# Narrower transposes, splits and reciprocals in the second attention of an audio tower kernel

## The chip, the cores and the metric

The kernel runs on one core of a Trainium2 chip. The metric is the device time of one execution in microseconds. Three runs of the kernel before give a median of 673.44 us (673.26 to 674.73). The engines are named as in the profile: PE is TensorE (PEld its loads of the stationary operand), DVE VectorE, ACT ScalarE, POOL GpSimd, SP SyncE.

## What is computed

The input x is 128 clips of 90 channels and 750 samples. Each clip is cut into 46 patches of 16 samples, embedded to 192 features, and passed through a causal attention of one head and then through an attention of 12 heads of 16 features whose query, key and value projections get a top-2 mixture of 8 low-rank adapters. Cut to what matters here:

```python
h = tok(x, W, b)                                  # (128, 46, 192)
h = h + attn(layernorm(h), Wq, Wk, Wv)            # causal, one head
# second attention, on y = layernorm(h):
qkv = y @ W_qkv.T + b_qkv + adapters(y)           # top 2 of 8, rank 16
q, k, v = split into 12 heads of 16
p = softmax(q @ k.T * 16 ** -0.5)                 # (128, 12, 46, 46)
out = (p @ v) as (128, 46, 192)
return h + out @ W_proj.T + b_proj
```

## The kernel before

The 128 clips are worked on in 16 groups of 8 clips, and within a group in 4 pairs of clips (`PAIRS`). The program of every engine is a loop over 24 steps (`STEPS`). One step holds one instance of every operation, in an order written out by hand at the end of each engine's `step`, and each operation works on the group `s - LAG[op][n]`, so up to nine groups are in flight at different stages. An operation whose group lies outside 0 to 15 is left out: the first steps fill the pipeline, the last ones drain it. The engines run their own lists in order and meet only at semaphores. Products are taken in fp16 with a high and a low part (three matmuls for one product, L1220 to L1222, five in `deep_product`, L1228), so nearly every tensor that is carried from PSUM to SBUF is written twice: its high part by ACT (`copy`, L680), and its low part, source minus high part, by DVE (`low`, L948).

The part that the change touches is the second attention's softmax and its product with the values. For each pair of clips p:

- `s_(p)` (PE, L1424) writes scores with the two clips' queries on partitions 0 to 63 and 64 to 127 (46 of each 64, `SLOT`, are real) and 12 heads of 46 keys in a row.
- `max2`, `shift` (DVE, L959 and L967) and `exp2` (ACT, L720) make the probabilities p2, [128, 12, 64], of which columns 46 to 63 of each head are zero from the start.
- `p_(p)` (PE, L1436): six fp32 transposes of 128 rows by two heads, into the two PSUM banks of ps_p. The operand p2 is the stationary one, the identity the moving one.
- `p2t(p)`: ACT copies ps_p (768 numbers in a row) to p2T's high part in fp16 (L680), then DVE makes its low part (L948). There is one p2T and one ps_p, so PE waits for `p2T_ready` before it transposes the next pair, and `pv(p)` waits for it too.
- `pv(p)` (PE, 18 matmuls at L1220 to L1222): both clips of the pair and a column of ones, so that the sums of the probabilities come with the product.
- `norm2(p)` (DVE): two reciprocals of those sums, one for each clip's 64 rows (L987), then two multiplications into o2 (L991).
- `ot(kh)` (PE, L1466): four fp32 transposes of o2, 128 rows each, for each of two halves; its parts are split as o2T by `o_high` and `o_low`, and go to the projection `pr`.

PE's order around this, from its list of a step (other work between):

```python
p_(3); g_(0); tok(9); g_(1); tok(10); pv(3); at(); tok(11); s_(0); ot(0); sc(); ot(1); s_(1)
qk_(0); qk_(1); qk_(2); p_(0); pt(); cv(0); av(0); av(1); s_(2); pr(0); xt(0); tok(0) ... tok(3); pv(0); p_(1)
```

Ahead of the loop stands a prologue: weights are loaded, transposed and split, and pads and masks are cleared by memsets on DVE and POOL. The last DVE memsets (`v2_room`, L941, and q3's pad, L942) stand directly ahead of step 0. In the prologue p2T serves as the room of a weight product (`qk_T`).

Of the kernel before, what the change touches and what calls it, by code (L numbers as in the profile page):

```python
# [14 lines left out]
NT = T // PATCH  # L15
# [23 lines left out]
RUN = EXTRA  # L39
SLOT = 64  # L40
PAD = 128 - PT_

# [37 lines left out]
def audio_tower(nc, x, tok_W, tok_b, Wq, Wk, Wv, W_qkv, b_qkv, W_gate, b_gate, A, B_lora,  # L80
                W_proj, b_proj, out, scratch):
    with ExitStack() as ctx:
# [118 lines left out]
        s_w = sem("weights_loaded")  # L201
        s_ident = sem("ident_ready")
        s_zero = sem("pads_cleared")
        s_maskf = sem("mask_ready")
# [184 lines left out]
        HP_DMAS = 6  # L389

        def v2_split(n, part):

            return (v2s[:, n, :, :, :, part, 0:HD].rearrange("p s a h e -> p (s a h) e"), heads_of(bank(f"cv{n}")[0:PT_, 0:2 * D]))
# [7 lines left out]
        def _(sp):  # L401
# [35 lines left out]
            def step(s):  # L437
# [40 lines left out]
                def stack_qk():  # L478
                    g = group(s, "stack_qk")
                    if g is not None:  # L480
                        if g == 0:
                            sp.wait_ge(s_wz, 4)
                        sp.wait_ge(s_scw, g * 32 + 32)
                        if g > 1:
                            sp.wait_ge(p_s, (g - 1) * PAIRS)
                        half = SLOT * (g % 2)
                        for n, (qp, kp) in enumerate(((0, 0), (1, 0), (0, 1))):
                            sp.dma_start(q3[half + HD * n:half + HD * (n + 1), :, 0:TG], w_out[g % 2, qp, :, 0:HEADS, :]).then_inc(s_qk3, 16)
                            sp.dma_start(k3[half + HD * n:half + HD * (n + 1), :, :], w_out[g % 2, kp, :, HEADS:2 * HEADS, :]).then_inc(s_qk3, 16)

                def place_v2():
                    g = group(s, "place_v2")
                    if g is not None:
                        if g == 0:
                            sp.wait_ge(s_wz, 4)
                        if g > 1:
# [29 lines left out]
        def _(pool):  # L526
# [23 lines left out]
            pool.wait_ge(s_ident, 1)  # L550
            nc.gpsimd.tensor_copy(ident_b[:], ident[0:PT_, 0:PT_]).then_inc(s_maskf, 1)
            pool.wait_ge(s_maskf, 7)
            for p in range(PAIRS):
# [124 lines left out]
        def _(act):  # L678
# [34 lines left out]
            def step(s):  # L713
# [8 lines left out]
                def p2t(p):  # L722
                    g = group(s, "p2t_high", p)
                    if g is not None:
                        act.wait_ge(p_p, g * PAIRS + (p + 1))
                        if g + p:
                            act.wait_ge(p_pv, g * PAIRS + p)
                        copy(p2T[:, 0].rearrange("p (a b) c -> p a (b c)", a=2), ps_p[:, :, 0:3 * 128]).then_inc(s_p2h, 1)

# [175 lines left out]
        def _(dve):  # L905
# [33 lines left out]


            nc.vector.memset(v2_room, 0.0).then_inc(s_wz, 1)  # L941
            nc.vector.memset(q3[0:SLOT + 3 * HD, :, TG:], 0.0).then_inc(s_wz, 1)  # L942

            def step(s):
# [26 lines left out]
                def p2t(p):  # L971
                    g = group(s, "p2t_low", p)
                    if g is not None:
                        low(p2T[:, 1].rearrange("p (a b) c -> p a (b c)", a=2), ps_p[:, :, 0:3 * 128],
                            p2T[:, 0].rearrange("p (a b) c -> p a (b c)", a=2), 1.0, s_p2h, g * PAIRS + (p + 1), s_p2T)

                def norm2(p):

                    g = group(s, "norm2", p)
                    if g is not None:  # L980
                        dve.wait_ge(p_pv, g * PAIRS + (p + 1))
                        if g:
                            dve.wait_ge(p_ot, g * 2)
                        pv = bank(f"pv{p}")[:, 0:HEADS * 2 * (HD + 1)].rearrange("p (b h e) -> p b h e", b=2, e=HD + 1)
                        for b in range(2):
                            r = slice(SLOT * b, SLOT * (b + 1))
                            nc.vector.reciprocal(rc[r, p, :], pv[r, b, :, HD]).then_inc(s_rc, 1)  # L987
                        for b in range(2):
                            r = slice(SLOT * b, SLOT * (b + 1))
                            dve.wait_ge(s_rc, g * PAIRS * 2 + (2 * p + 1 + b))  # L990
                            nc.vector.tensor_tensor(o2[r, p, 0:D].rearrange("p (h e) -> p h e", h=HEADS), pv[r, b, :, 0:HD],  # L991
                                                    rc[r, p, :].unsqueeze(2).to_broadcast([SLOT, HEADS, HD]),
                                                    ALU.mult).then_inc(s_o2, 1)
# [221 lines left out]
        def _(pe):  # L1215
# [45 lines left out]
            def step(s):  # L1261
# [166 lines left out]
                def p_(p):  # L1428
                    g = group(s, "p", p)
                    if g is not None:  # L1430
# [3 lines left out]
                        for half in range(2):  # L1434
                            for a in range(3):
                                last = nc.tensor.transpose(ps_p[:, half, 128 * a:128 * (a + 1)],  # L1436
                                                           p2[:, 6 * half + 2 * a:6 * half + 2 * a + 2, :].rearrange("p a b -> p (a b)"),
                                                           ident[:])
                        last.then_inc(p_p, 1)
# [17 lines left out]
                def ot(kh):  # L1457
                    g = group(s, "ot", kh)
                    if g is not None:
# [5 lines left out]
                        for p in range(PAIRS):  # L1465
                            last = nc.tensor.transpose(bank(f"ot{kh}")[:, 128 * p:128 * (p + 1)], o2[:, p, DA * kh:DA * (kh + 1)], ident[:])  # L1466
                        last.then_inc(p_ot, 1)
# [63 lines left out]


def f32_of(ap):

# [33 lines left out]
```

## Time and profile before

| | us |
|---|---|
| median of 3 runs | 673.44 (673.26 to 674.73) |
| the profiled execution's own time | 675.54 |
| its span, first to last instruction | 673.8 |
| PE busy | 602.9 (89% of the span) |
| DVE busy | 509.0 (76%) |
| POOL busy | 380.8 (57%) |
| ACT busy | 367.0 (54%) |
| mean granted TensorE clock | 0.953 of full speed |

The lists of the engines repeat every 34.0 us in the middle of the span, so the span falls into a prologue (to about 57 us), steps that fill the pipeline (to about 157 us), full steps (to about 558 us), and steps that drain it. In a row of the trace, "a<-b" is what is written and what is read (buffer numbers left out), the shapes are partitions x elements per partition, and for a matmul the form "128*128 128x128" gives rows and columns of the stationary operand and then rows and columns of the moving one. "Idle before" is how long the engine stood still just ahead of the instruction, and the arrow names what ended that.

### The profile page before, as it was taken

Reading aid. Unit: us, or ns where it says so; the run is one execution under the profiler, and the core shown is the slowest. Engines: PE = TensorE matmul, PEld = TensorE weight load, DVE = VectorE, ACT = ScalarE, POOL = GpSimd, SP = SyncE. Lnnn points to the kernel's source line nnn. Section 1 sums busy time; section 2 is a strip of 40 time slices with the busy share of each in tenths; the row PEclk is TensorE's granted clock in tenths of the full one; section 3 lists DMA queues with packets and bytes.
Section 4 is the critical chain, followed back from the end, with each engine's and each line's share of the span. In section 5 each row is a group of like instructions: output and inputs, shape, how many; then the busy total and the mean of one; then the engine's idle time right before and its main releaser. Section 6 shows DMA issues by size and latency. Waiting matters only on the chain.

```text
span 673.8 us, 20478 instructions
## 1 busy us (share of the span) xinstructions
PE 602.9 (89%) x7805; PEld 537.4 (80%) x7805; DVE 509.0 (76%) x1369; ACT 367.0 (54%) x688; POOL 380.8 (57%) x649
## 2 busy tenths in 40 slices
PE   1597779989999999999999999999999998877673
PEld 1367668879898989898989898989898987766563
DVE  4324145677888888888888888888888888887772
ACT  2524455556666666666666666666666454533231
POOL 5608768876767676767666666767675323121100
PEclk9999779998999999999999999999999998987876
DMA  8843564968494949494949494949492616161500
GB/s 207 148 94 82 120 149 96 156 171 138 124 159 136 159 134 159 135 159 135 150 141 155 138 166 128 173 123 167 131 167 65 108 32 104 36 105 37 94 23 17
DMA packets 74930, 82.94 MB, mean 123 GB/s; under 512 B 10093, under 2 KB 60241, under 8 KB 74833
## 3 DMA queue, kind: packets, MB, share of 16 engines
q1 hardware_dynamic: 74832, 81.63, 59.5%
q8 instruction: 62, 1.02, 0.7%
q14 instruction: 36, 0.29, 0.2%
HBM read 50.24 MB, written 13.57 MB: 95 GB/s over the span
## 4 chain that ended last, share of the span: by engine, by line
PE 78%; DVE 7%; POOL 6%; SPq 4%; issue 3%; ACT 1%; DMA 0%; POOLq 0%; DVEq 0%; ACTq 0%
PE ps_r L1228 23%; PE ps_tok L1220 7%; PE ps_tok L1221 6%; PE ps_tok L1222 6%; PE ps_p L1436 6%; PE ps_s L1424 4%; PE ps_r L1220 4%; PE ps_r L1222 4%; SPq L403 4%; PE ps_r L1221 4%; PE ps_r L1466 3%; PE ps_r L1346 3%; POOL xs L588 3%; PE ps_r L1289 2%; PE ps_r L1359 1%
## 5 line engine op out<-in xcount | busy, mean ns | idle before, releaser
L588 POOL TENSOR_TENSOR xs<-raw,xs 90x368 f16<-90x368 f32 x192 | 163.9, 881 | 19.8 <-ACT xs L680 19.8
L1220 PE MATMUL ps_tok<-w_tok,xs 128*128 128x192 f16 x576 | 146.2, 254 | 1.2 <-DVE h L1003 1.2
L1221 PE MATMUL ps_tok<-w_tok,xs 128*128 128x192 f16 x576 | 145.9, 253 | 0.0
L1222 PE MATMUL ps_tok<-w_tok,xs 128*128 128x192 f16 x576 | 145.8, 253 | 0.0
L680 ACT ACTIVATE p2T<-ps_p 128x768 f16<-128x768 f32 x64 | 51.8, 810 | 72.3 <-PE ps_p L1436 57.5
L680 ACT ACTIVATE xs<-raw 90x736 f16<-90x736 f32 x96 | 75.6, 805 | 0.1
L596 POOL TENSOR_TENSOR ad<-ga,disp 128x384 f32<-128x384 f32 x16 | 13.4, 839 | 105.8 <-DVE disp L1058 105.8
L588 POOL TENSOR_TENSOR xe<-raw,xe 90x368 f16<-90x368 f32 x64 | 55.6, 881 | 28.2 <-ACT xe L680 28.2
L1220 PEld LDWEIGHTS ps_tok<-w_tok,xs 128*128 128x128 f16 x576 | 66.8, 116 | 4.2 <-POOL xs L588 1.1
L1221 PEld LDWEIGHTS ps_tok<-w_tok,xs 128*128 128x128 f16 x576 | 66.8, 116 | 1.7
L1222 PEld LDWEIGHTS ps_tok<-w_tok,xs 128*128 128x128 f16 x576 | 66.8, 116 | 0.3
L948 DVE SCALAR_TENSOR_TENSOR p2T<-ps_p,p2T 128x768 f16<-128x768 f32 x64 | 60.7, 949 | 3.9 <-ACT p2T L680 2.9
L1220 PE MATMUL ps_r<-v,p2T 128*128 128x68 f16 x384 | 46.7, 202 | 16.2 <-DVE p2T L948 14.2
L1436 PE MATMUL ps_p<-ident,p 128*128 128x128 f32 x384 | 56.7, 287 | 2.4 <-DVE p2T L948 2.0
L1220 PEld LDWEIGHTS ps_r<-v,p2T 128*128 128x128 f16 x384 | 38.7, 101 | 17.6 <-DVE p2T L948 16.0
L987 DVE RECIPROCAL rc<-ps_r 64x12 f32<-64x12 f32 x128 | 29.5, 230 | 30.6 <-PE ps_r L1222 27.0
L991 DVE TENSOR_TENSOR o<-ps_r,rc 64x192 f32<-64x192 f32 x128 | 45.5, 356 | 4.0
L1436 PEld LDWEIGHTS ps_p<-ident,p 128*128 128x128 f32 x384 | 44.8, 147 | 4.3 <-issue 2.7
L1222 PE MATMUL ps_r<-v,p2T 128*128 128x68 f16 x384 | 46.8, 201 | 0.0
L1221 PE MATMUL ps_r<-v,p2T 128*128 128x68 f16 x384 | 46.8, 201 | 0.0
L967 DVE TENSOR_TENSOR df<-ps_s,mx 128x552 f32<-128x552 f32 x64 | 46.2, 722 | 0.7
L959 DVE TENSOR_REDUCE mx<-ps_s 128x12 f32<-128x552 f32 x64 | 46.1, 720 | 0.2 <-PE ps_s L1424 0.2
(163 smaller groups left out, 1614.0 us busy)
## 6 DMA issues: line engine op xcount, KB each, us to landing
raw<-x SPq DMA_DIRECT2D x32, 1035.0 KB, 7.9
qk_scratch<-qk SPq DMA_DIRECT2D x32, 276.0 KB, 3.0
q<-qk_scratch SPq DMA_DIRECT2D x48, 138.0 KB, 7.0
k<-qk_scratch SPq DMA_DIRECT2D x48, 138.0 KB, 7.7
xs<-xe SPq DMA_DIRECT2D x32, 184.0 KB
v<-v2s SPq DMA_DIRECT2D x64, 73.3 KB
out<-h2b SPq DMA_DIRECT2D x16, 276.0 KB
xs<-xe SPq DMA_DIRECT2D x16, 149.5 KB
```

The costliest lines, as they stand in the source:

```text
L588: nc.gpsimd.tensor_tensor(lo, src, hi, ALU.subtract).then_inc(s_lo, 1)
L680: return nc.scalar.activation(out_, in_, ACT.Copy, scale=scale)
L948: nc.vector.scalar_tensor_tensor(out=out_, in0=src, scalar=scale, in1=hi, op0=ALU.mult, op1=ALU.subtract).then_inc(done, 1)
L959: nc.vector.tensor_reduce(mx[:].rearrange("p (a h) -> p a h", a=2), scores2(), AX_X, ALU.max).then_inc(s_mx, 1)
L967: nc.vector.tensor_tensor(df[:].rearrange("p (a h) k -> p a h k", a=2), scores2(), mx[:].rearrange("p (a h) -> p a h", a=2).unsqueeze(3).t ...
L987: nc.vector.reciprocal(rc[r, p, :], pv[r, b, :, HD]).then_inc(s_rc, 1)
L991: nc.vector.tensor_tensor(o2[r, p, 0:D].rearrange("p (h e) -> p h e", h=HEADS), pv[r, b, :, 0:HD], rc[r, p, :].unsqueeze(2).to_broadcast([ ...
L1220: mm(dst, stat[0], mov[0], start=start, stop=False)
L1221: mm(dst, stat[0], mov[1], start=False, stop=False)
L1222: return mm(dst, stat[1], mov[0], start=False, stop=stop)
L1228: last = mm(dst, stat(a), mov(b), start=start and n == 0, stop=stop and n == 4)
L1436: last = nc.tensor.transpose(ps_p[:, half, 128 * a:128 * (a + 1)], p2[:, 6 * half + 2 * a:6 * half + 2 * a + 2, :].rearrange("p a b -> p ( ...
```

## The change

The 46 rows of each clip stand at partitions 0 to 45 and 64 to 109, so the last real row is 109 of 128; ROWS is 64 + 46 = 110. The change does four things:

1. The transposes `p_` and `ot` take 110 rows in place of 128. The stationary operand keeps its 128 columns; the moving identity shrinks from 128 to 110 columns.
2. `p2t` splits only the 46 used of each 64 columns: 12 x 46 = 552 numbers per partition in place of 768, on ACT and on DVE. DVE's instruction becomes a plain subtraction. The columns that are no longer written are cleared once in the prologue, by a DVE memset of p2T, and ACT waits for it (`s_wz` of 3).
3. `norm2` takes one reciprocal over 110 rows for both clips, and multiplies 46 rows for each clip. The column of ones stands in the values of both clips, so the sums in the first clip's block of `pv` are those of every row, and the one reciprocal reads that block alone.
4. o2's rows 46 to 63, which are now read by `ot` but never written, are cleared once by a POOL memset in the prologue, and DVE waits for it.

```diff
+ROWS = SLOT + NT
...
+        def p2T_used(part):
+
+            return used(p2T[:, part].rearrange("p (a b) (c q) -> p a (b c) q", a=2, q=SLOT))
+
+        def ps_p_used():
+            return used(ps_p[:, :, 0:3 * 128].rearrange("p a (b q) -> p a b q", q=SLOT))
...
             nc.gpsimd.tensor_copy(ident_b[:], ident[0:PT_, 0:PT_]).then_inc(s_maskf, 1)
+            nc.gpsimd.memset(o2[:], 0.0).then_inc(s_o2z, 1)
...
                         act.wait_ge(p_p, g * PAIRS + (p + 1))
+                        act.wait_ge(s_wz, 3)
                         if g + p:
                             act.wait_ge(p_pv, g * PAIRS + p)
-                        copy(p2T[:, 0].rearrange("p (a b) c -> p a (b c)", a=2), ps_p[:, :, 0:3 * 128]).then_inc(s_p2h, 1)
+                        copy(p2T_used(0), ps_p_used()).then_inc(s_p2h, 1)
...
+            nc.vector.memset(f32_of(p2T[:]), 0.0).then_inc(s_wz, 1)
             nc.vector.memset(v2_room, 0.0).then_inc(s_wz, 1)
...
-                        low(p2T[:, 1].rearrange("p (a b) c -> p a (b c)", a=2), ps_p[:, :, 0:3 * 128],
-                            p2T[:, 0].rearrange("p (a b) c -> p a (b c)", a=2), 1.0, s_p2h, g * PAIRS + (p + 1), s_p2T)
+                        dve.wait_ge(s_p2h, g * PAIRS + (p + 1))
+                        nc.vector.tensor_tensor(p2T_used(1), ps_p_used(), p2T_used(0), ALU.subtract).then_inc(s_p2T, 1)
...
+                        nc.vector.reciprocal(rc[0:ROWS, p, :], pv[0:ROWS, 0, :, HD]).then_inc(s_rc, 1)
+                        dve.wait_ge(s_rc, g * PAIRS + (p + 1))
+                        dve.wait_ge(s_o2z, 1)
                         for b in range(2):
-                            r = slice(SLOT * b, SLOT * (b + 1))
-                            nc.vector.reciprocal(rc[r, p, :], pv[r, b, :, HD]).then_inc(s_rc, 1)
-                        for b in range(2):
-                            r = slice(SLOT * b, SLOT * (b + 1))
-                            dve.wait_ge(s_rc, g * PAIRS * 2 + (2 * p + 1 + b))
+                            r = slice(SLOT * b, SLOT * b + NT)
                             nc.vector.tensor_tensor(o2[r, p, 0:D].rearrange("p (h e) -> p h e", h=HEADS), pv[r, b, :, 0:HD],
-                                                    rc[r, p, :].unsqueeze(2).to_broadcast([SLOT, HEADS, HD]),
+                                                    rc[r, p, :].unsqueeze(2).to_broadcast([NT, HEADS, HD]),
                                                     ALU.mult).then_inc(s_o2, 1)
...
-                                last = nc.tensor.transpose(ps_p[:, half, 128 * a:128 * (a + 1)],
-                                                           p2[:, 6 * half + 2 * a:6 * half + 2 * a + 2, :].rearrange("p a b -> p (a b)"),
-                                                           ident[:])
+                                last = nc.tensor.transpose(ps_p[:, half, 128 * a:128 * a + ROWS],
+                                                           p2[0:ROWS, 6 * half + 2 * a:6 * half + 2 * a + 2, :].rearrange("p a b -> p (a b)"),
+                                                           ident[0:ROWS, 0:ROWS])
...
-                            last = nc.tensor.transpose(bank(f"ot{kh}")[:, 128 * p:128 * (p + 1)], o2[:, p, DA * kh:DA * (kh + 1)], ident[:])
+                            last = nc.tensor.transpose(bank(f"ot{kh}")[:, 128 * p:128 * p + ROWS], o2[0:ROWS, p, DA * kh:DA * (kh + 1)],
+                                                       ident[0:ROWS, 0:ROWS])
...
+def used(ap):
+    return ap[..., 0:NT]
```

Two waits of SP on `s_wz` go from 4 to 5, for the memset that was added. No instruction changes its place in an engine's list. On DVE, at the end of a full step, the list before reads (rc and o are the reciprocals and the normalised output of `norm2`, the rows from lg to disp the router's ranking and dispatch):

```order
L948 SCALAR_TENSOR_TENSOR p2T<-ps_p,p2T 128x768
L1003 SCALAR_TENSOR_TENSOR h<-ps_tok,b_tok_bc 128x192
L1032 TENSOR_TENSOR lg<-ga,b_gate_bc 128x24
L1034 TENSOR_REDUCE top<-lg 128x3
L1035 TENSOR_TENSOR lgm<-lg,top 128x24
L1041 TENSOR_TENSOR ahead<-lg 128x192
L1043 TENSOR_TENSOR over<-ahead,beats 128x192
L1045 TENSOR_REDUCE rank<-over 128x24
L987 RECIPROCAL rc<-ps_r 64x12 x2
L991 TENSOR_TENSOR o<-ps_r,rc 64x192 x2
```

and the list of the changed kernel at the same place:

```order
L987 TENSOR_TENSOR p2T<-ps_p,p2T 128x12x46
L1014 SCALAR_TENSOR_TENSOR h<-ps_tok,b_tok_bc 128x192
L1043 TENSOR_TENSOR lg<-ga,b_gate_bc 128x24
L1045 TENSOR_REDUCE top<-lg 128x3
L1046 TENSOR_TENSOR lgm<-lg,top 128x24
L1052 TENSOR_TENSOR ahead<-lg 128x192
L1054 TENSOR_TENSOR over<-ahead,beats 128x192
L1056 TENSOR_REDUCE rank<-over 128x24
L997 RECIPROCAL rc<-ps_r 110x12
L1002 TENSOR_TENSOR o<-ps_r,rc 46x192 x2
```

The neighbours stay; one reciprocal is gone, and the split is of 552 numbers.

## Rows read from the trace of the kernel before

**Rows 1.** The page: engines' busy time, and TensorE's granted clock in 40 slices
```profile
PE 602.9 (89%) x7805; PEld 537.4 (80%) x7805; DVE 509.0 (76%) x1369; ACT 367.0 (54%) x688; POOL 380.8 (57%) x649
...
PEclk9999779998999999999999999999999998987876
```

**Rows 2.** Windows: us, busy (x count) of PE, PEld, DVE, ACT, POOL, clock, DMA
```profile
157.00:558.00 401.00, 399.94 (x5660) 365.42 (x5657) 354.00 (x975) 254.33 (x476) 262.52 (x443) 1.00 0.66 136
562.00:674.00 112.00, 80.77 (x1058) 68.96 (x1058) 79.87 (x183) 38.22 (x69) 14.70 (x22) 0.81 0.33 58
```

**Rows 3.** Waits, 562 to 674 us: us in total, times, longest us
```profile
PE ps_r L1220 <- DVE p2T L948: 14.2, 7, 3.4
...
DVE rc L987 <- PE ps_r L1222: 8.5, 9, 1.3
```

**Rows 4.** The chain that ended last, 562 to 674 us: shares by line
```profile
by line: PE ps_r L1228 14.4%; PE ps_p L1436 9.2%; DVE p2T L948 8.6%; PE ps_r L1466 6.2%; issue 6.2%; PE ps_r L1220 5.2%; DVE o L991 4.7%; PE ps_r L1222 4.3%; PE ps_r L1221 4.2%; DVE rc L987 4.1%; PE ps_s L1424 3.4%; POOL xn L629 1.7%; PE ps
```

**Rows 5.** The chain, 200 to 300 us: start us, us, what
```profile
278.40 0.46 PE ps_r L1466 x4
...
297.85 0.32 PE ps_r L1359 x4
...
298.92 0.66 PE ps_p L1436 x6
```

**Rows 6.** Groups by form, 157 to 562 us: xcount | busy us, mean ns
```profile
L1436 PE MATMUL ps_p<-ident,p 128*128 128x128 f32 x288 | 40.0, 275 | 0.0
...
L1466 PE MATMUL ps_r<-ident,o 128*128 128x128 f32 x96 | 15.3, 282 | 0.0
```

**Rows 7.** Groups by form, the whole span
```profile
L948 DVE SCALAR_TENSOR_TENSOR p2T<-ps_p,p2T 128x768 f16<-128x768 f32 x64 | 60.7, 949 | 3.9 <-ACT p2T L680 2.9
...
L680 ACT ACTIVATE p2T<-ps_p 128x768 f16<-128x768 f32 x64 | 51.8, 810 | 72.3 <-PE ps_p L1436 57.5 <-PE ps_r L1222 13.5
...
L967 DVE TENSOR_TENSOR df<-ps_s,mx 128x552 f32<-128x552 f32 x64 | 46.2, 722 | 0.7
...
L991 DVE TENSOR_TENSOR o<-ps_r,rc 64x192 f32<-64x192 f32 x128 | 45.5, 356 | 4.0
...
L720 ACT ACTIVATE p<-df 128x552 f32<-128x552 f32 x64 | 42.0, 657 | 0.0
...
L987 DVE RECIPROCAL rc<-ps_r 64x12 f32<-64x12 f32 x128 | 29.5, 230 | 30.6 <-PE ps_r L1222 27.0
...
L1003 DVE SCALAR_TENSOR_TENSOR h<-ps_tok,b_tok_bc 128x192 f32<-128x192 f32 x48 | 16.7, 349 | 19.3 <-PE ps_tok L1222 19.2
```

**Rows 8.** Groups by form, 562 to 674 us
```profile
L987 DVE RECIPROCAL rc<-ps_r 64x12 f32<-64x12 f32 x32 | 7.3, 229 | 9.1 <-PE ps_r L1222 8.5
```

**Rows 9.** The chain, 640 to 674 us: start us, us, what
```profile
651.79 0.23 DVE rc L987
...
652.05 0.25 DVE rc L987
...
656.59 0.82 ACT p2T L680
...
657.43 0.97 DVE p2T L948
```

**Rows 10.** Timeline to 62 us: start us, us, instruction [idle before]
```profile
15.01 1.73 POOL L588 TENSOR_TENSOR xe<-raw,xe 90x368 f16<-90x368 f32 x2 [5.91 <-ACT xe L680]
...
54.72 2.78 DVE L941 MEMSET v<- 128x3264 f32 x1 [0.63 <-issue]
...
58.28 0.36 DVE L1003 SCALAR_TENSOR_TENSOR h<-ps_tok,b_tok_bc 128x192 f32<-128x192 f32 x1 [0.55 <-PE ps_tok L1222]
...
59.08 0.18 DVE L1016 BATCH_NORM_AGGREGATE mv<-st 128x2 f32<-128x6 f32 x1
...
58.79 0.25 PE L1220 MATMUL ps_tok<-w_tok,xs 128*128 128x192 f16 x1 [0.54 <-DVE h L1003]
...
61.84 0.19 POOL L566 TENSOR_TENSOR ve<-mv,eps 128x1 f32<-128x1 f32 x1
```

More of the change, by code:

```diff
@@ L202, in audio_tower @@
         s_ident = sem("ident_ready")
+        s_o2z = sem("o2_cleared")
         s_zero = sem("pads_cleared")
@@ L481, in stack_qk @@
                         if g == 0:
-                            sp.wait_ge(s_wz, 4)
+                            sp.wait_ge(s_wz, 5)
                         sp.wait_ge(s_scw, g * 32 + 32)
@@ L494, in place_v2 @@
                         if g == 0:
-                            sp.wait_ge(s_wz, 4)
+                            sp.wait_ge(s_wz, 5)
                         if g > 1:
```

## The prediction

> **What bounds the kernel now.** I read the page first. PE is busy for 89% of the span and DVE for 76%, and TensorE's clock is at full speed from about a fifth of the span to nine tenths of it, below that only at both ends [rows 1]. Shares over the whole span do not say where an edit pays, so I read the windows next. From 157 to 558 us PE is busy for 399.94 of 401 us at clock 1.00, while DVE is busy for 354 and ACT for 254 [rows 2]. There PE's own list is the limit, and only what shortens PE shortens the kernel. From 562 to 674 us PE is busy for 80.77 of 112 us at a mean clock of 0.81, and DVE for 79.87: neither fills the time [rows 2]. The waits of that stretch say why: PE stood 14.2 us in seven waits for DVE's p2T, and DVE 8.5 us in nine waits for PE's product before a reciprocal [rows 3]. So the drain is a chain p_, high part on ACT, low part on DVE, pv, reciprocal, and each link counts. The chain that ended last gives the links their weight in these 112 us: transposes p_ 9.2% and ot 6.2%, DVE's p2T 8.6%, reciprocals 4.1% [rows 4].
>
> **Part 1, the transposes.** In the full steps PE works back to back, so what counts is the spacing from one instruction to the next, which the chain shows, not an instruction's own length, which overlaps its neighbours. Six p_ transposes take 0.66 us, 110 ns each with 128 moving columns, and four ot transposes 0.46 us, 115 ns each. The transposes of xn2 (L1359) are the same kind of instruction, fp32 with a stationary operand of 128 columns, but 92 rows and so 92 moving columns: four take 0.32 us, 80 ns each [rows 5]. From 128 to 92 is 36 columns for 30 ns, 0.83 ns a column; 18 columns fewer give 15 ns. For one instruction the ends are nothing (the spacing is set by the stationary load) and the whole step to the 92-column row, 30 ns. I take 15, because 110 lies halfway between two rows of the same kind; the 30 would need the whole step to come in its first half. Between 157 and 562 us there are 288 p_ and 96 ot transposes [rows 6]: 384 x 15 ns = 5.8 us, all of it on the path, for PE has no idle time to give. In the drain the chain holds (9.2% + 6.2%) of 112 us = 17.2 us of transposes [rows 4], part of it at half clock, where a column costs twice as much; 18 of 128 columns of that are 2.4 us.
>
> One rule speaks against this part. The Trainium skill, TensorE: Matmul & The Clock Gate, section Back-to-back issue gap, says that in a stream of weight loads and matmuls the spacing is set by both, and its section on LDWEIGHTS lets a load take as long as the stationary operand has columns, by its formula 107 ns for 128 of them. The stationary operand keeps its 128 columns here, so by that rule this part would give nothing, and the sum below would be 4.2 us in place of 12.0. The trace is against it, since the 92-column transposes have 128 stationary columns and still follow each other at 80 ns [rows 5]; I keep the row's price and make the rule's case a rival.
>
> **Part 2, the split on 552 numbers.** DVE's low part takes 949 ns for 768 numbers. A DVE subtraction that reads 552 fp32 numbers from PSUM takes 722 ns [rows 7]. I take 722 for the new one: 227 ns less. ACT's high part takes 810 ns for 768; the nearest ACT row with 552 numbers in runs of 46 is exp2's, 657 ns [rows 7]: 153 ns less. That exp2 costs so little with its output in runs of 46 is also why I charge nothing for runs. In the full steps both gains are worth nothing: PE is never kept waiting there [rows 2]. What covers them is PE's own list; without that cover DVE would be the next limit, at 354 of 401 us. In the drain the chain holds 8.6% of 112 = 9.6 us of DVE's low parts [rows 4]; 227 of 949 of that is 2.3 us. ACT's high parts are on the chain twice (the row at 656.59 is one of the two) [rows 9]: 0.3 us.
>
> **Part 3, one reciprocal.** A reciprocal on 64 rows x 12 takes 230 ns; it runs over the free dimension, and rows cost nothing: DVE's h<-ps_tok on 128 rows x 192 takes 349 ns, the o multiplication on 64 rows x 192 takes 356 ns [rows 7]. So one on 110 rows takes 230 ns, the multiplications on 46 rows keep their 356 ns, and of the drain's 32 reciprocals 16 are dropped [rows 8]. On the chain they stand as two pieces in a row, 0.23 and 0.25 us [rows 9], 4.1% of 112 = 4.6 us in all [rows 4]; half of it is 2.3 us. The first multiplication now directly follows the reciprocal that it needs. Before, the second one stood so too, and no gap of more than 0.03 us separates the chain's pieces there, so I charge nothing. In the full steps this is covered as in part 2.
>
> **Part 4, the memsets.** DVE clears 128 x 3264 fp32 in 2.78 us, 0.85 ns an element, so p2T's 768 take 0.65 us, just ahead of step 0. DVE then stood idle 0.55 us until PE's first embedding tile was done, so h is late by 0.1 us, and PE, which waited 0.54 us for it, starts its next tile as much later. The next who needs it is POOL, whose layer norm at 61.84 us comes after its own queue of splits and reads what DVE had at 59.3 us [rows 10]. Ends: nothing and 0.65 us; I take nothing. POOL's memset of o2, 1024 elements, costs some 0.9 us by the same price, ahead of a wait of 5.91 us for the first input [rows 10]: nothing. SP's waits for one more count and ACT's and DVE's new waits are for memsets of the prologue, 90 us before the first p_, and nobody queues behind them.
>
> **The sum.** Full steps 5.8 us. Drain 2.4 + 2.3 + 0.3 + 2.3 = 7.3 us if every link of the chain gives all it has. It will not: where a link is shortened another path comes up, for instance DVE's mx or h2b pieces that already stand directly ahead of a low part. I take 85%, 6.2 us; the ends are 1 us (other paths take over at once) and 7.3 us. In all 12.0 us. The profiled execution has a span of 673.8 and its own time is 675.54; less 12.0 that is 661.8 and 663.5. The median of the runs lies 2.1 us below the profiled one, so I forecast 673.44 - 12.0 = **661.4 us**.
>
> **Rivals.**
> - *The drain is held by something else.* Layer norm 2 on POOL, ACT's copies and half-clock PE stretches are in the same 112 us. Then the full steps' 5.8 us and 1 us remain: 666.6 us. Against: seven waits for p2T itself. Chance 0.11.
> - *The stationary load sets the transposes' spacing.* Parts 2 and 3 alone, 85% of 4.9 us: 673.44 - 4.2 = 669.2 us. For it: nothing but that the stationary operand stays at 128 columns; against: the 80 ns row. It is the case that the Trainium skill's rule above describes. Chance 0.08.
> - *The change doesn't do what it says on the split:* the pattern of 2 x 6 runs of 46 costs ACT and DVE as much as 768 in a row. Then 2.6 us of the drain go, 85% of it 2.2 us: 663.6 us. Against: exp2 writes the same runs. Chance 0.04.
> - *Slower: TensorE's clock in the drain.* The granted clock there is 0.81 on average, that is a mix of 2.4 and 1.2 GHz, in a stretch where PE often stands waiting. The PE entries named in the chain's row add up to 47% of it, 52 us [rows 4], or 52 x 0.81 = 42 us of work at full clock. If the new rhythm of waits lowers the mean to c, that work takes 42/c. It eats the whole 12 us at c = 0.66 and leads to 677 us at 0.62. For it: the last tenth of the span already has 0.6 and 0.7 in places [rows 1]. Against: the change shortens the very stretches in which PE waits. Chance 0.03.
>
> **How the numbers follow.** My forecast has 0.74, with its own range from 657 to 665: 13.1 us if the drain gives all, and a few us more if the drain's clock rises (42/0.88 is 4 us less than 52). A run of this kernel can tell about 0.2%, 1.35 us, from no change. Everything but the last rival is faster by more than that: faster 0.95, within 0.2% 0.02 (a partial form of the last rival), slower 0.03. For the range I go from 657 to 669.5, which takes in the first three rivals and leaves out the last, the outer tails and the 30 ns end of part 1 (653 us).
>
> **What would show it.** In the profile after: a p_ group spaced at 0.57 us and an ot group at about 0.40 us on the chain; a period of 33.5 us in place of 34.0 with PE still busy all through; DVE's p2T near 722 ns and ACT's near 650; 64 reciprocals of 110x12 at 230 ns; the wait of PE for p2T in the drain down from 14.2 by some 3 us. An unchanged period would prove the stationary-load rival, a shorter period with an unchanged 112 us drain the first one. I would be wrong altogether if PE showed idle time in the full steps, or a clock below 1.00 there.

## The result, and the profile after

| | before | after |
|---|---|---|
| median, us | 673.35 (670.48 to 674.73, 4 runs) | 662.52 (661.36 to 664.97, 4 runs) |
| ratio after / before, 95% interval | | 0.9849 (0.9807 to 0.9892) |
| the profiled execution's own time | 675.54 | 661.36 |
| its span | 673.8 | 659.6 |
| mean granted clock | 0.953 | 0.956 |

The forecast was 661.4 us with a range from 657.0 to 669.5; the kernel takes 662.5. It is faster by 10.8 us, where 12.0 were expected. Below are the rows of the changed kernel that answer to [rows 1 to 7, 10].

The page of the changed kernel, busy time and granted clock:

```profile
PE 592.3 (90%) x7805; PEld 527.3 (80%) x7805; DVE 484.4 (73%) x1306; ACT 356.0 (54%) x688; POOL 382.0 (58%) x650
...
PEclk9999789998999999999999999999999999996875
```

PE is 10.6 us less busy for the same 7805 instructions, DVE 24.6 us less for 63 fewer (64 reciprocals less, one memset more). Taken over the whole span, DVE's saving is more than twice what the kernel gained. Where it counted only the stretches tell.

Windows of the changed kernel, full steps and then drain, with the columns of [rows 2]:

```profile
157.00:552.00 395.00, 393.46 (x5639) 359.51 (x5637) 335.29 (x926) 245.93 (x476) 261.29 (x442) 1.00 0.67 137
556.00:660.00 104.00, 76.78 (x1055) 64.39 (x1051) 72.71 (x167) 35.55 (x69) 14.35 (x22) 0.80 0.35 62
```

PE is still busy for 99.6% of the full steps at clock 1.00, so its list is the limit there as before. DVE's share fell from 88% to 85%, and the period doesn't follow it (e2, e3 and e4 below).

Chain of the changed kernel in full steps (start us, us, what), which answers to [rows 5]:

```profile
291.99 0.32 PE ps_r L1370 x4
...
295.69 0.57 PE ps_p L1447 x6
...
308.82 0.40 PE ps_r L1477 x4
```

Six p_ transposes are spaced 95 ns apart where it was 110, four ot 100 where it was 115; xn2's, which the change doesn't touch, still take 80.

Groups by form, whole span (busy us, mean ns | idle before):

```profile
L1447 PE MATMUL ps_p<-ident,p 110*128 110x110 f32 x384 | 49.6, 267 | 1.8 <-DVE p2T L987 1.2 <-ACT p L730 0.4
L987 DVE TENSOR_TENSOR p2T<-ps_p,p2T 128x552 f16<-128x552 f32 x64 | 46.3, 723 | 3.1 <-ACT p2T L690 2.2
L1002 DVE TENSOR_TENSOR o<-ps_r,rc 46x192 f32<-46x192 f32 x128 | 45.5, 355 | 4.2
L690 ACT ACTIVATE p2T<-ps_p 128x552 f16<-128x552 f32 x64 | 40.3, 630 | 64.3 <-PE ps_p L1447 53.1 <-PE ps_r L1233 10.3
```

The split on DVE costs 723 ns (949 before), on ACT 630 (810 before); the multiplication costs the same on 46 rows as on 64. The reciprocal on 110 rows has 64 instructions of 232 ns, 14.8 us in all.

Waits in the drain, 556 to 660 us (us in total, times, longest), beside [rows 3]:

```profile
PE ps_r L1231 <- DVE p2T L987: 11.1, 7, 3.1
...
DVE rc L997 <- PE ps_r L1233: 7.5, 8, 1.3
```

**Where the time went.** As a milestone I take the first reciprocal of the first attention (`rl`, DVE) in each step: it has one fixed place in DVE's list, so the distance from one to the next is the period of a step, and the milestones cut the span into fill, twelve full steps, and drain. The same cut is used for every kernel below.

| us, in the profiled executions | before | after |
|---|---|---|
| start to the third milestone | 149.7 | 147.9 |
| twelve full steps | 408.6 | 404.0 |
| period of an undisturbed full step | 33.88 | 33.42 |
| drain | 115.5 | 107.7 |
| span | 673.8 | 659.6 |

The period is 0.46 us shorter, which is 5.5 us over twelve steps. (The 34.0 us named ahead of the prediction are 33.88 when measured this way.) Twelve periods are less than the second line: in every kernel the first of the twelve steps and the eleventh take 0.8 to 1.6 us longer than the period (in one kernel, with filler, the first takes 3.3 us longer). Two things in the table are scatter and no effect: the first line varies between 147 and 150 us among all kernels with no order to it, and other single steps take 0.3 to 2 us longer (more in the last section). So the profiled pair shows 14.2 us, while the medians show 10.8.

### The profile page after: what moved, and what is told of

Same layout as the page of the kernel before. It is cut to its first block, busy times and chain, and to the rows that moved or that the text cites. A ratio compares the mean times of both kernels' runs of the same rounds, so it can differ in the third digit from the quotient of the medians.

```text
span 659.6 us, 20481 instructions
## 1 busy us (share of the span) xinstructions
PE 592.3 (90%) x7805; PEld 527.3 (80%) x7805; DVE 484.4 (73%) x1306; ACT 356.0 (54%) x688; POOL 382.0 (58%) x650
## 4 chain that ended last, share of the span: by engine, by line
PE 77%; DVE 7%; POOL 5%; SPq 4%; issue 3%; ACT 2%; DMA 0%; POOLq 0%; DVEq 0%
PE ps_r L1239 24%; PE ps_tok L1231 7%; PE ps_tok L1232 7%; PE ps_tok L1233 7%; PE ps_p L1447 5%; PE ps_s L1435 4%; PE ps_r L1231 4%; SPq L412 4%; PE ps_r L1233 4%; PE ps_r L1232 4%; PE ps_r L1357 3%; POOL xs L598 2%; PE ps_r L1477 2%; PE ps_r L1300 2%; PE ps_r L1370 1%
## 5 line engine op out<-in xcount | busy, mean ns | idle before, releaser
L690 ACT ACTIVATE p2T<-ps_p 128x552 f16<-128x552 f32 x64 | 40.3, 630 | 64.3 <-PE ps_p L1447 53.1
L1231 PE MATMUL ps_r<-v,p2T 128*128 128x68 f16 x384 | 45.8, 200 | 13.4 <-DVE p2T L987 11.1
L1447 PE MATMUL ps_p<-ident,p 110*128 110x110 f32 x384 | 49.6, 267 | 1.8 <-DVE p2T L987 1.2
L1231 PEld LDWEIGHTS ps_r<-v,p2T 128*128 128x128 f16 x384 | 38.1, 100 | 14.4 <-DVE p2T L987 12.8
L987 DVE TENSOR_TENSOR p2T<-ps_p,p2T 128x552 f16<-128x552 f32 x64 | 46.3, 723 | 3.1 <-ACT p2T L690 2.2
L1002 DVE TENSOR_TENSOR o<-ps_r,rc 46x192 f32<-46x192 f32 x128 | 45.5, 355 | 4.2
L850 ACT ACTIVATE xn<-h,nb,rs 128x192 f32<-128x192 f32 x48 | 26.1, 543 | 40.1 <-POOL nb L621 40.1
L1239 PE MATMUL ps_r<-x2T,w_qk 128*128 128x368 f16 x240 | 46.9, 327 | 0.0
L1233 PE MATMUL ps_r<-v,p2T 128*128 128x68 f16 x384 | 45.8, 199 | 0.0
L1232 PE MATMUL ps_r<-v,p2T 128*128 128x68 f16 x384 | 45.7, 199 | 0.0
```

Of the source, the lines that this page charges most:

```text
L690: return nc.scalar.activation(out_, in_, ACT.Copy, scale=scale)
L987: nc.vector.tensor_tensor(p2T_used(1), ps_p_used(), p2T_used(0), ALU.subtract).then_inc(s_p2T, 1)
L1231: mm(dst, stat[0], mov[0], start=start, stop=False)
L1232: mm(dst, stat[0], mov[1], start=False, stop=False)
L1233: return mm(dst, stat[1], mov[0], start=False, stop=stop)
L1239: last = mm(dst, stat(a), mov(b), start=start and n == 0, stop=stop and n == 4)
```

## Experiments

Every ratio is to the kernel before, run beside it on the same chip. The medians of before were 672.9 us (24 runs) beside e1, e2, e3 and e4, 674.4 (11 runs) beside a1, e7, e8 and f12, and 673.9 (26 runs) beside the rest. "Gain" below is the ratio applied to 673.4 us. The first question is how the gain is divided among the parts, since my sum gave each of them a size.

### e1: the transposes alone

```diff
-    transpose(ps_p[:, half, 128 * a:128 * (a + 1)], p2[:, ...], ident[:])
+    transpose(ps_p[:, half, 128 * a:128 * a + ROWS], p2[0:ROWS, ...], ident[0:ROWS, 0:ROWS])
-    transpose(bank(f"ot{kh}")[:, 128 * p:128 * (p + 1)], o2[:, ...], ident[:])
+    transpose(bank(f"ot{kh}")[:, 128 * p:128 * p + ROWS], o2[0:ROWS, ...], ident[0:ROWS, 0:ROWS])
```

The split stays at 768 numbers and there are two reciprocals, now on 46 rows each; o2 and ps_p are cleared once.

> The transposes of part 1 alone (p_ and ot on 110 rows); the split stays on 768 numbers and there are two reciprocals, on 46 rows each; ps_p and o2 are cleared once in the prologue. My theory (PE's list is the limit of the full steps, a column costs 0.83 ns): the period falls from 33.9 to 33.4 us, the stretch up to the drain shrinks by about 6 us and the drain by about 2 us, median about 665.5 us. Rival (the stationary load sets the spacing): period and median unchanged, 673.3 us. Rival (the drain's gain came from DVE alone): 6 us, all of it before the drain, about 667.5 us.

Measured: 670.87 us (7 runs), ratio 0.9948 (0.9924 to 0.9972), a gain of 3.5 us. The period is 33.42 us, all of the change's 0.46. The drain takes 114.7 us, hardly less than before. The 665.5 us expected before the run are missed by 5.4.

### e2: the split alone

```diff
-    copy(p2T[:, 0]..., ps_p[:, :, 0:3 * 128])
+    copy(p2T_used(0), ps_p_used())
-    low(p2T[:, 1]..., ps_p[:, :, 0:3 * 128], p2T[:, 0]..., 1.0, ...)
+    nc.vector.tensor_tensor(p2T_used(1), ps_p_used(), p2T_used(0), ALU.subtract)
...
```

Transposes on 128 rows, two reciprocals on 46 rows.

> Part 2 alone: the split on 552 of 768 numbers, its memset and waits; transposes on 128 rows, two reciprocals, on 46 rows each. My theory: DVE's 227 ns and ACT's 180 ns a pair are hidden in the full steps, so the period stays at 33.9 us, and the drain gives about 2.2 us: median about 671.1 us. Rival (DVE's time counts everywhere): 64 x 0.227 = 14.5 us, 659 us. Rival (the drain is held by other paths): 673.3 us.

Measured: 669.27 us (12 runs), ratio 0.9937 (0.9911 to 0.9962), a gain of 4.2 us (1.7 either way). Period 33.88 us, as before; drain 109.8 us.

### e3: the reciprocal alone

```diff
+    nc.vector.reciprocal(rc[0:ROWS, p, :], pv[0:ROWS, 0, :, HD])
     for b in range(2):
-        nc.vector.reciprocal(rc[r, p, :], pv[r, b, :, HD])
...
```

> Part 3 alone: one reciprocal on 110 rows, multiplications on 46 rows; transposes and split as before. My theory: period unchanged, about 2.0 us from the drain, median about 671.4 us. Rival (DVE's time counts everywhere): 64 x 0.23 = 14.7 us, 658.7 us. Rival (the wait for the one reciprocal, which no second one covers any more, gives it back): 673.3 us or a little over.

Measured: 672.03 us (12 runs), ratio 0.9984 (0.9962 to 1.0006), a gain of 1.1 us that its interval doesn't tell from none. Period 33.88 us; the profiled execution, 1.8 us below this kernel's median, has a drain of 109.7.

### e4: split and reciprocal together, transposes as before

> Parts 2 and 3 together, so the whole change but the transposes. My theory: period unchanged, 4.2 us from the drain (5 if the two add up without loss), median about 669.2 us, and the difference to the changed kernel, 662.5 us, is the transposes' 6.7. Rival (the parts shorten the same link twice, or another path takes over): no more than the larger of parts 2 and 3 alone, about 671 us.

Measured: 668.24 us (6 runs), ratio 0.9922 (0.9892 to 0.9953), a gain of 5.3 us, which is e2's and e3's together. Period 33.88 us, drain 108.6.

### a1: the changed kernel again

> The changed kernel once more, unedited, beside the others of this call. Additive parts would put it at the transposes' step of the first call (0.52% less than before) plus that of parts 2 and 3 (0.78%): 1.30%, 664.2 us. If the parts help each other (the transposes alone lengthened the half-clock time of the drain, the split takes it back), it is below that: 1.5% as measured at first, 662.8 us.

Measured: 663.14 us (6 runs), ratio 0.9841 (0.9804 to 0.9878), a gain of 10.7 us; period 33.42, drain 107.4 us. The result repeats. The parts add up to 8.8 us (e1's 3.5 and e4's 5.3), or to 10.1 with e1's repeat below (4.8). The intervals are 1.6 to 2.5 us either way, so they don't tell whether the parts merely add or help each other.

### e0: the memsets and their waits alone

```diff
+    nc.vector.memset(f32_of(p2T[:]), 0.0).then_inc(s_wz, 1)
     nc.vector.memset(v2_room, 0.0).then_inc(s_wz, 1)
...
+    nc.gpsimd.memset(o2[:], 0.0).then_inc(s_o2z, 1)
```

> The kernel before with the two new memsets and their waits alone (p2T cleared by VectorE 0.70 us before the loop, o2 by POOL 0.95 us). Theory, as in the prediction: no change, 672 to 675 us, since xt waits for weights that come at 71.5 us and VectorE's first h, though 0.8 us later, is done long before. Rival: the later start of VectorE goes through to the end, 0.84 us, 0.1 per cent; then the first rl of the first step comes 0.8 us later and the time is 0.8 us more, which the interval of such a run would hardly tell, but the milestones of the trace would.

Measured: 674.83 us (10 runs), ratio 1.0005 (0.9977 to 1.0033). The timeline of this kernel's prologue (start us, us, instruction):

```profile
54.71 0.70 DVE L944 MEMSET p2T<- 128x768 f32 x1
...
59.20 0.36 DVE L1008 SCALAR_TENSOR_TENSOR h<-ps_tok,b_tok_bc 128x192 f32<-128x192 f32 x1
```

The first h starts 0.92 us later than in [rows 10]. Its first milestone is at 91.84 us, where before had 93.26, but that milestone lies anywhere between 91.2 and 93.3 us in the kernels of this document, so it can't show what became of a delay of this size. The ratio shows no cost, with an interval of 1.9 us either way. This kernel does before's work otherwise, so it is also a second look at before: its drain took 113.7 us, against 115.5. So two profiled drains of the same work can differ by 1.8 us. Of that, 1.5 us lie in the drain's first step, which took 30.76 us here at a granted clock of 1.00 and 32.27 us in before at 0.95.

### What became of the transposes' share in the drain

e1's drain was 0.8 us shorter in the profile, where I had counted on 2.0, and its median left the drain no gain at all (3.5 us, with 5.5 from the full steps). The clock was one suspect, since e1's last stretch ran at 0.71 of full speed and before's at 0.76. I repeated e1 beside a kernel that differs from it by matmuls that nobody needs:

```diff
+    if s >= 19 and k in (3, 7, 8, 10):
+        pe.wait_ge(s_h, GROUPS * 3)
+        for _ in range(12):
+            mm(ps_tok[:, 0:D], xs[:, 0, 0, 0, 0:128, 0], w_tok[:, 0, 0, :], start=True, stop=True)
```

The moving operand of these matmuls has 192 columns (`D`); the text before the run says 96.

> The kernel with the narrower transposes alone, and 12 more matmuls of 96 columns at four of the tok slots of every step from the 19th on, on data that has long been there. Their result is overwritten by the tok matmuls that follow, so nothing of the output changes. The question is why the transposes alone gave 3.5 us of the 7.8 expected. Theory A, the granted clock: with less for TensorE to do in the drain, the clock stays low for longer there and takes back what the transposes give. Then this kernel's drain shows a higher clock than that of the transposes alone (0.71 in its last 84 us), its last stretch is shorter than 84.1 us by some 2 to 4 us, and the time is 667 to 668, if the filler's own work (48 matmuls a step of about 0.05 us, of which part lies in waits) does not eat it. Theory B, the drain of the transposes alone is bound by the wide split on VectorE, and the clock has no part: the last stretch stays at 84 us or grows by the filler's work, and the time is 671 to 673.

> The transposes p_ and ot on 110 rows alone, once more, beside the one with filler on the same chip. Expected as before: 0.9948 of the kernel before, 670 to 671 us; full steps of 33.42 us, and a last stretch of 83 to 85 us at a clock near 0.71. If the last stretch comes out at 79 to 80 us instead, at a clock of 0.76 or more, then the small gain of the first run was scatter of the clock, and no lasting trait of this kernel; the time is then 666 to 667.

Measured: with filler 668.92 us (12 runs), ratio 0.9938 (0.9915 to 0.9961); without it 669.22 us (9 runs), ratio 0.9929 (0.9896 to 0.9962). The windows of the drain, cut at its first whole step, without and with filler (clock third from the end):

```profile
552.62:584.71 32.09, 27.26 (x373) 22.79 (x372) 28.14 (x72) 16.60 (x33) 6.81 (x12) 0.95 0.42 74
584.71:667.30 82.59, 54.64 (x728) 46.38 (x726) 55.54 (x128) 23.87 (x41) 8.41 (x12) 0.73 0.29 53
```

```profile
554.88:586.76 31.88, 28.31 (x385) 24.15 (x384) 27.94 (x71) 16.63 (x33) 6.79 (x12) 0.95 0.42 73
586.76:670.10 83.34, 69.12 (x956) 60.73 (x954) 55.56 (x128) 23.86 (x41) 8.43 (x12) 0.88 0.30 53
```

The filler adds 228 matmuls and 14.5 us of busy PE to the last stretch and lifts the clock from 0.73 to 0.88, and the stretch is 0.75 us longer, not 2 to 4 us shorter. PE's wait for p2T falls from 13.8 to 5.0 us with it: part of the filler lies in that wait. That is theory B's outcome in the trace, though its 671 to 673 us were not measured, and the medians don't tell the two kernels apart.

What it rules out is that a higher clock, bought in this way, returns anything. It doesn't decide whether the clock ate the transposes' share, for the filler has a price of its own. In the chain of this kernel's last stretch it stands with 5.5 us ahead of the last output (and 5.9 us more beside the writing of it), yet the stretch grew by only 0.75 us. By that estimate the rest of it is 4.7 us shorter, which the higher clock would explain. More numbers point to the clock. e1's 16 executions ran at a mean clock of 0.938 to 0.956, before's 61 beside all the runs at 0.951 to 0.963. Twice (1 - clock) times the span is an estimate of the time at half clock, and gives 67 to 71 us for e1, 58 to 59 for before, and 41 for e1 with filler. PE's busy time in the last stretch didn't fall with the narrower transposes: 56.7 and 54.6 us in e1's two traces, at 0.71 and 0.73, against 55.5 in before and 55.3 in e0, at 0.76 and 0.74. And the drain's first step, with the same work, took 30.59 us in e1's first trace, at 1.00, and 32.09 us in its repeat, at 0.95, as with e0 and before.

The same filler on the changed kernel:

> The changed kernel with 12 matmuls of 192 columns, whose result nobody reads, ahead of pv(0), pv(2), pv(3) and behind pv(1) in steps 19 to 23, where PE otherwise stands waiting. Clock theory (the transposes' gain in the drain is eaten because a PE with less to do runs at half clock for longer): the mean clock rises from 0.956 to 0.97 or more, the 78 us at 0.74 become 72 or so, median about 657 us in spite of the added work. Rival (the drain's length is set by DVE's and ACT's work, the clock is a bystander): the filler only delays PE, 662.5 to 668 us.

Measured: 662.74 us (6 runs), ratio 0.9832 (0.98 to 0.9864), the changed kernel's own time, at a clock of 0.85 in the last stretch in place of a1's 0.77. In the profiled pair that stretch is 3.3 us longer with filler (81.4 against 78.1), so here too nothing speaks for it. This profiled execution is the slowest of its six, 2.7 us above their median, and that of e1 with filler is 2.9 us above its own.

The other candidate is in the chain. Here is the drain's chain of e1's repeat, by line:

```profile
by line: PE ps_r L1233 14.5%; DVE p2T L952 9.2%; PE ps_p L1442 6.5%; issue 6.4%; DVE o L996 5.3%; PE ps_r L1225 5.0%; DVE rc L992 4.4%; PE ps_r L1472 4.4%; PE ps_r L1227 4.2%; PE ps_r L1226 4.0%; PE ps_s L1429 2.8%; DVE mx L963 2.3%; DVE h 
```

and here the waits of PE for p2T in the drain in it, in e2 and in the changed kernel run again:

```profile
PE ps_r L1225 <- DVE p2T L952: 13.8, 7, 3.5
```

```profile
PE ps_r L1232 <- DVE p2T L986: 12.0, 7, 3.2
```

```profile
PE ps_r L1231 <- DVE p2T L987: 11.1, 7, 3.1
```

Summed up by engine from the pieces of each drain's chain:

| us on the chain of the drain | PE | DVE | drain |
|---|---|---|---|
| before | 57.0 | 38.1 | 115.5 |
| e0 | 54.3 | 39.1 | 113.7 |
| e1 | 53.3 | 41.6 | 114.7 |
| e1, again | 50.4 | 43.8 | 114.7 |
| e2 | 52.5 | 36.8 | 109.8 |
| e3 | 54.1 | 35.8 | 109.7 |
| e4 | 54.9 | 32.7 | 108.6 |
| after | 49.2 | 36.7 | 107.7 |
| a1 | 50.3 | 35.6 | 107.4 |

With narrower transposes PE's part of the chain shrinks, and DVE's grows in its place: p2T, mx and df stand on it longer. PE's wait for p2T stays at 14 us (13.8, beside [rows 3]) and shrinks only where the split is narrower. From e4 to after it is the same trade: PE 5.7 us less, DVE 4.0 more. I read this as two paths of nearly equal length, one through PE's transposes and one through DVE's list, with DVE's the longer: DVE's savings come through and PE's mostly don't. Against the mean of before and e0, 114.6 us, e1 saves nothing, and the transposes on top of e4 save about 1 us. That reading is argued from the chains and not shown: no run holds the clock and changes the path, or the other way round. So whether the second path or the lower clock took the transposes' share, or both, stays open.

### e7: the stationary operand narrowed too

The rival of the stationary load is tested here. p_ takes 110 columns of p2 as the stationary operand in place of 128, and the split runs on 110 partitions.

```diff
-    transpose(ps_p[:, half, ...], p2[0:ROWS, ...].rearrange("p a b -> p (a b)"), ident[0:ROWS, 0:ROWS])
+    transpose(ps_p[0:ROWS, half, ...], p2[0:ROWS, ...].rearrange("p a b -> p (a b)")[:, 0:ROWS], ident[0:ROWS, 0:ROWS])
```

> The changed kernel with 110 in place of 128 columns in the stationary operand of p_ (and the split on 110 partitions). My theory (the moving columns set the spacing): a group of six stays at 0.57 to 0.59 us and the period at 33.42 us, the median at 662.5. Rival (the stationary load still sets part of it): down to 0.50 us a group, a period shorter by up to 0.3 us, median down to 659 us.

Measured: 662.18 us (4 runs), ratio 0.9835 (0.9792 to 0.9878), a1's time. Groups by form of this kernel:

```profile
L1447 PE MATMUL ps_p<-ident,p 110*110 110x110 f32 x384 | 49.8, 268 | 1.0 <-ACT p L730 0.4 <-DVE p2T L987 0.3
...
L1447 PEld LDWEIGHTS ps_p<-ident,p 110*110 110x110 f32 x384 | 39.5, 138 | 2.9 <-issue 1.1 <-ACT p L730 0.5
```

The load is named 138 ns instead of 145 and the spacing is still 0.57 us for six; the period is 33.40 us. The width of the stationary operand doesn't set it. Whether it is the moving columns or the rows (both went from 128 to 110) wasn't tried: the identity of a transpose is square, so the two can't be parted here.

### e8: pv in two passes

PE waits in the drain for the low part, while two thirds of pv's matmuls need only the high part. This kernel starts those first:

```diff
-    pe.wait_ge(s_p2T, g * PAIRS + (p + 1))
+    pe.wait_ge(s_p2h, g * PAIRS + (p + 1))
...
+        for part in range(2):
+            mm(dst[:, :, 2 * j:2 * j + 2, :], p2T[:, 0, j, :], v2[:, g % 2, :, :, p, j, part, :], start=j == 0 and part == 0, stop=False)
+    pe.wait_ge(s_p2T, g * PAIRS + (p + 1))
+    for j in range(HEADS // 2):
+        mm(dst[:, :, 2 * j:2 * j + 2, :], p2T[:, 1, j, :], v2[:, g % 2, :, :, p, j, 0, :], start=False, stop=j == HEADS // 2 - 1)
```

> The changed kernel with pv in two passes: the 12 matmuls that need only p2T's high part go ahead of the wait for the low part, the 6 with the low part behind it. If the chain p_, high, low, pv, reciprocal bounds the drain: of 7 waits of PE for p2T each is shorter by up to the 0.4 us (0.65 at half clock) of the 12 matmuls, so the drain gives 2 to 4 us, and the full steps nothing: median about 659.5 us. If what that wins is lost to the clock as with the transposes alone: no change, 662.5 us.

Measured: 661.16 us (660.54 to 661.78, 6 runs), ratio 0.9811 (0.9783 to 0.9838). That is 2.0 us below a1 beside it; the intervals overlap, but the drain is also shorter, 104.5 us against 107.4, so I take it for a gain. It falls short of the 659.5 us that were expected. The wait on the low part and the chain of this kernel's drain:

```profile
PEld ps_r L1466 <- DVE p2T L987: 4.6, 7, 2.0
```

```profile
by line: PE ps_r L1239 17.0%; DMA v<-v2s 7.4%; issue 6.9%; PE ps_p L1447 5.7%; SPq L510 5.2%; DVE p2T L987 4.6%; DVE o L1002 3.9%; PE ps_s L1435 3.0%; PE ps_r L1462 2.5%; PE ps_r L1479 2.4%; DVE h L1105 2.3%; PE ps_r L1466 2.2%; DVE st L111
```

The load's wait for the low part is 4.6 us where the changed kernel's was 12.8. That isn't 8 us won: the load now also waits 4.6 us, in five waits, for the high part from ACT, which the old order hid behind the low part, so 3.6 us of waiting are gone and 2.9 us come out of the drain. The DMA that places v2, with its queue on SP, has come up as a new link (12.6% of the chain), where it had no place before.

### e9: e8 and the other transposes with spare rows

xt and at take their second tile on 112 rows instead of 128.

> The changed kernel with two more edits: pv starts its matmuls on the high parts before it waits for the low parts (the edit of e8_two_pass_pv), and the transposes xt and at take their second tile on its 112 rows instead of 128. Of these there are 9 calls a step, one of the three tiles of each 16 moving columns narrower: 9 x 16 x 0.83 ns = 0.12 us a step by the 0.83 ns a column that the two widths of p_ and ot showed, which is 1.9 us over 16 steps. If the list of TensorE sets the full steps, the period goes from 33.42 to 33.30 us and the time from 661.2 to 659.5 us, 0.978 of before. If the spacing of these calls is set by what they wait for, the period stays at 33.42 and the time at 661.

Measured: 661.02 us (6 runs), ratio 0.9805 (0.9774 to 0.9836), e8's time. Its drain took 105.8 us, 1.6 less than a1's where e8's was 2.9 less, so what the two passes save in a profiled drain is known no better than that. The text before the run counted three times too many: only one tile in three is narrower, two of xt's six transposes in a step and one of at's three, which makes 3 x 16 x 0.83 ns = 0.04 us a step. The period is 33.40 us against 33.42, but e7, without this edit, has 33.40 too, so the 0.04 us can't be read from it. e8 and e9 are the best of all that ran; between them the runs don't decide.

## Why the prediction was right, point by point

- **Full steps, 5.8 us expected, 5.5 shown.** The period fell by 0.46 us for 32 transposes, 14.4 ns each against the 15 that I took between the two rows of [rows 5]. It falls by that (in e7 and e9 by 0.48) in each kernel with narrower transposes, and stays at 33.88 us in each without. PE is still busy throughout.
- **Splits and reciprocals nothing in the full steps.** Right: e2, e3 and e4 have before's period.
- **The drain, 6.2 us expected in all.** The medians leave 10.8 - 5.5 = 5.3 us for it; the profiled pair shows 7.8, of which up to 1.8 is scatter by e0. The total was right and its division wrong, so there is luck in the total. The transposes' term, 2.4 us before the cut to 85%, was too big: e1's two medians give 3.5 and 4.8 us for the whole kernel (1.6 and 2.2 either way), less than the full steps alone. The splits' term of 2.6 us (DVE's 2.3, ACT's 0.3) looks too small: e2 gives 4.2 us, though its interval goes down to 2.5. The reciprocals' 2.3 us looks too big, though it lies within e3's interval: e3 gives 1.1 (1.5 either way), and from e2 to e4 it is 1.1 again. The step that failed is the reading of [rows 4] as a price list. The chain's shares say what each link holds, and not what shortening it returns. Why the transposes returned less, a DVE path beside them or the lower clock, is open. e2's executions ran at a higher clock than before's beside it (0.957 to 0.965 against 0.951 to 0.963), which may be how the split returned more than its share. My cut of 15% was the right idea, spread over the wrong terms.
- **Durations.** DVE's split at 722 ns came out at 723, ACT's at 657 came out at 630, the reciprocal at 230 at 232, the multiplication unchanged. On DVE runs of 46 cost nothing extra (723 ns, and 722 for the subtraction of [rows 7]), and rows nothing either (232 ns on 110, 230 on 64).
- **The waits.** PE's for p2T fell from 14.2 to 11.1 us, the 3 that were named.
- **The memsets.** They cost nothing that e0's ratio shows, as was forecast. I wrote that h would be late by 0.1 us, since DVE had stood idle 0.55 us ahead of it, waiting for PE's first embedding tile. In the changed kernel it came 0.84 us later, with 0.60 us of idle time still ahead of it:

```profile
54.18 0.70 DVE L952 MEMSET p2T<- 128x768 f32 x1
...
58.52 0.32 PE L1233 MATMUL ps_tok<-w_tok,xs 128*128 128x192 f16 x1
...
58.83 0.25 PE L1233 MATMUL ps_tok<-w_tok,xs 128*128 128x192 f16 x1
...
59.12 0.36 DVE L1014 SCALAR_TENSOR_TENSOR h<-ps_tok,b_tok_bc 128x192 f32<-128x192 f32 x1 [0.60 <-PE ps_tok L1233]
```

  But the memset isn't what made it late. PE's tile was late: its last matmul ended at 59.08 us (58.25 in before), because PE's matmuls stood 0.16 us apart, at half clock, until 58.67 us, and in before only until 56.93; from there they stand 0.08 us apart. In the kernels with the same memsets whose clock rose early (56.82 us in e8, 56.13 in e4), h follows the memsets with no idle time, at 58.53 and 58.29 us against 58.28 in before. So the idle time was slack, and the memset of 0.70 us used it up, about as the prediction had it. Behind it there is more: the first transposes of xt start at 71.46 us in the changed kernel, and at 71.50 in before.
- **The rival of the stationary load** fell: by it the ratio would have been 0.9937, and the period unchanged. The Trainium skill, TensorE: Matmul & The Clock Gate, section Back-to-back issue gap, sets the spacing of a stream of loads and matmuls by both; by its formula, an estimate, 128 stationary columns would hold these transposes at 107 ns. The trace doesn't agree: with 128 stationary columns they stand 95 ns apart, and with 110 (e7) the same.
- **The rival of a drain held by something else** fell as a whole, since the drain did get shorter, but for one part of three, the transposes, something else did hold it. **The flat pattern** fell with the 723 ns. **The clock** was 0.74 in the last stretch against 0.76 and didn't make the kernel slower; what it took from the transposes is the open question above.

## What to carry to other kernels

Cut the span by a milestone that comes once a step and read each stretch for itself: in the full steps only the list of the engine that never waits counted, and in the drain DVE's narrower split counted and PE's narrower transposes hardly. A chain's share is no price for a link: here one link returned less than its share promised and another, by its median, more. Before pricing it, look for the path that runs beside it and for what the shorter work does to TensorE's clock, and repeat the profile, since two drains of the same work differ. When a consumer waits for the last of several inputs, as pv did for the low part, order its work so that what needs the earlier inputs goes first, and expect the next links (here the high part from ACT, and a DMA) to take part of the gain.

## What was unexpected

- **fp32 transposes are priced by the 128, 110 or 92 on their moving side, and finely:** 110, 95 and 80 ns apart, 0.83 ns for each column, the same whether the stationary operand has 128 or 110 columns.
- **Lone stalls of PE in the full steps.** A step now and then takes 0.3 to 2 us more than its period. In a1 and e2 the trace shows, between 325 and 340 us, one stall of PE each that it can put down to nothing:

```profile
PE ps_r L1239 <- issue: 1.4, 1, 1.4
```

```profile
PE ps_r L1240 <- issue: 1.7, 1, 1.7
```

  Steps longer than the period come in every kernel, two always at the same place (the first and the eleventh of the twelve), others anywhere. Their cause stays open. They aren't all that makes single executions scatter by 5 us and more: before's slower executions mostly have the lower mean clock too (669.5 us at 0.963 and 678.3 at 0.951, the ends of the 24 beside e1), which time added at full clock would not bring.
- **The clock of the drain can be lifted for nothing gained.** 12 useless matmuls at four places of each late step took it from 0.73 to 0.88, and the time didn't move. With 5.5 us of the filler itself on the chain, that doesn't say that the clock is worth nothing.
